# Attention: q and k of a steady turn are projected once, with even and odd columns crossed, and turned by adding halves of partitions

## The reference, cut to what matters

```
def rot(t):
    t = t.reshape(*t.shape[:-1], half, 2)
    t0, t1 = (t[..., 0], t[..., 1])
    r0 = t0 * cos - t1 * sin
    r1 = t1 * cos + t0 * sin
    return jnp.stack([r0, r1], axis=-1).reshape(*t0.shape[:-1], head_dim)
...
qkv = x @ qkv_w + qkv_b
...
q, k = _rope(q, k, S, D)
attn = jnp.einsum('bhqd,bhkd->bhqk', q, k) / math.sqrt(D)
attn = jax.nn.softmax(attn, axis=-1)
out = jnp.einsum('bhqk,bhkd->bhqd', attn, v)
return out @ out_w + out_b
```

## Time and profile before

| what | value |
|---|---|
| median of 3 runs | 1851.65 us |
| the profiled execution, first to last instruction (span) | 1847.4 us |
| so around the span | 4.25 us |
| TensorE's busy share of the span | 94% |
| VectorE, ScalarE, GpSimd | 78%, 76%, 77% |
| steady turns of the attention with a projection | 58 |

### The profile page before, as it was taken

How to read it: one execution, slowest core, us unless ns; L and a number is a source line. 1 busy time by engine, 2 the same in 40 slices (tenths; PEclk the granted TensorE clock), 3 DMA queues, 4 the chain that set the end, 5 groups by cost and what they waited for, 6 DMA issues and landing times. The chain is left out here.

```text
span 1847.4 us, 53971 instructions
## 1 busy us (share of the span) xinstructions
PE 1740.1 (94%) x22856; PEld 1101.7 (60%) x22856; DVE 1444.6 (78%) x2658; ACT 1407.5 (76%) x1737; POOL 1430.4 (77%) x851
## 2 busy tenths in 40 slices
PE   5999999999999999999999999986899999978997
PEld 2466666666666666666666666675556666653454
DVE  5888888888888888888888887535988888845785
ACT  2688888888888888888888888943998888853463
POOL 6699999999999999999999999974765566624122
PEclk9899999999999999999999999998999999989998
DMA  5101010111101010101010010050111111110000
GB/s 142 25 20 31 19 31 23 27 26 28 26 24 30 21 31 19 31 23 28 23 31 23 24 26 4 2 165 18 41 40 36 37 37 37 34 26 1 1 0 24
DMA packets 71080, 56.89 MB, mean 31 GB/s; under 512 B 29196, under 2 KB 64184, under 8 KB 70840
## 3 DMA queue, kind: packets, MB, share of 16 engines
q1 hardware_dynamic: 70840, 53.44, 11.5%
HBM read 14.54 MB, written 1.05 MB: 8 GB/s over the span
## 5 line engine op out<-in xcount | busy, mean ns | idle before, releaser
L278 POOL TENSOR_TENSOR ah_probs_lo<-ah_probs,ah_probs_hi 128x1024 f16<-128x1024 f32 x512 | 1072.8, 2132 | 78.8 <-ACT ah_probs L487 78.7
L542 DVE TENSOR_REDUCE ah_part_max<-ah_p_m 128x1 f32<-128x512 f32 x1024 | 669.2, 685 | 120.9 <-PE ah_p_m L342 111.1
L484 ACT ACTIVATE ah_probs_hi<-ah_p_s 128x1024 f16<-128x1024 f32 x512 | 531.2, 1038 | 190.0 <-PE ah_p_s L358 178.8
L487 ACT ACTIVATE ah_probs<-ah_p_s 128x1024 f32<-128x1024 f32 x512 | 532.4, 1040 | 0.0
L372 PE MATMUL ah_p_o<-ah_v_hi,ah_probs_hi 128*128 128x65 f16 x4096 | 470.5, 195 | 5.7 <-POOL ah_probs_lo L278 5.1
L374 PE MATMUL ah_p_o<-ah_v_lo,ah_probs_hi 128*128 128x64 f16 x4096 | 470.5, 193 | 0.0
L376 PE MATMUL ah_p_o<-ah_v_hi,ah_probs_lo 128*128 128x65 f16 x4096 | 470.3, 194 | 0.0
L372 PEld LDWEIGHTS ah_p_o<-ah_v_hi,ah_probs_hi 128*128 128x128 f16 x4096 | 383.0, 98 | 84.3 <-DVE a_attn L565 12.3
L374 PEld LDWEIGHTS ah_p_o<-ah_v_lo,ah_probs_hi 128*128 128x128 f16 x4096 | 378.4, 98 | 91.3
L342 PE MATMUL ah_p_m<-ah_k_hi_lo,ah_q_hi_twice 128*128 128x512 f16 x1024 | 393.9, 385 | 6.6 <-DMA ah_max_q_lo<-ah_lo 3.1
L357 PE MATMUL ah_p_s<-ah_q_hi_twice,ah_k_hi_lo 128*128 128x512 f16 x1024 | 388.6, 379 | 0.8 <-ACT ah_probs L487 0.4
(11 more groups left out here) (316 smaller groups left out, 3090.0 us busy)
## 6 DMA issues: line engine op xcount, KB each, us to landing
ba_v_skew<-ba_v_own SPq DMA_DIRECT2D x64, 129.0 KB, 2.3
ah_q_hi_twice<-ah_hi SPq DMA_DIRECT2D x128, 64.0 KB, 2.0
ah_k_hi_lo<-ah_hi SPq DMA_DIRECT2D x64, 64.0 KB, 1.9
ah_one_k_hi<-ah_hi SPq DMA_DIRECT2D x64, 64.0 KB, 2.0
ah_k_hi_lo<-ah_lo SPq DMA_DIRECT2D x64, 64.0 KB, 2.0
ah_max_q_lo<-ah_lo SPq DMA_DIRECT2D x64, 64.0 KB, 2.0
ah_w_head<-in_w_heads SPq DMA_DIRECT2D x16, 160.0 KB, 2.4
bw_rot<-in_rot SPq DMA_DIRECT2D x4, 512.0 KB, 10.3
```

The source lines that it names most:

```text
L278: pool.tensor_tensor(pl[:, p % RW, :, :], pb[:, p % RP, :, :], ph[:, p % RW, :, :], ALU.subtract).then_inc(lo_pool, 1)
L484: act.activation(ph[:, p % RW, :, :], p_s[:, p % 2, :, :], ACT.Exp, scale=HD ** -0.5)
L487: act.activation(pb[:, p % RP, :, :], p_s[:, p % 2, :, :], ACT.Exp, scale=HD ** -0.5).then_inc(exp_done, 1)
L542: dve.tensor_reduce(part[:, t, 2 * half + b:2 * half + b + 1], p_m[:, b, :], AX, ALU.max).then_inc(maxed, 1)
```

## The change

In the steady turns the 128 columns of a projection are crossed: 32 partitions each of q's even columns, k's odd columns, q's odd columns, k's even columns. Then what a partition needs from its partner stands 64 partitions away, in the same bank. One projection serves both products: step 0 projects (`W_CROSSED`) and multiplies by the sine into `rot`, step 1 multiplies by the cosine in place, step 2 adds `rot`'s upper half to `p_a`'s lower half (`cross_first`), and step 3 subtracts `rot`'s lower half from `p_a`'s upper half (`cross_second`). Rounding moves to steps 4 and 5, the row of maxima to step 6, the projection of v to step 7. Since q and k now lie in quarters, twelve DMAs of 32 partitions take the place of six of 64. The weights of a head have 7 x 64 columns for the first two heads, which also serve the early projections, and 3 x 64 after that; they had 5 x 64.

```
-W_COLS = 5 * HD
+QUAD = HD // 2
+W_COLS, W_LATER = 7 * HD, 3 * HD
...
+QE, KO, QO, KE = (slice(i * QUAD, (i + 1) * QUAD) for i in range(4))
...
+                    if g >= LEAD_G:
+                        sp.dma_start(ka[0:QUAD, to, cs], hi[KE, g % 2, :]).then_inc(spread[g % 2], 16)
+                        sp.dma_start(ka[QUAD:HD, to, cs], hi[KO, g % 2, :]).then_inc(spread[g % 2], 16)
...
                     if j == 0 and g <= LAST_G:
                         pe.wait_ge(vl_done, g)
-                        project(turned_bank(g), g, W_TURNED, turned_ready)
-                    if j == 1 and g <= LAST_G:
-                        pe.wait_ge(rot_done, g + 1)
-                        project(proj_bank(g), g, W_QK, proj_ready)
-                    if j == 5 and e + 1 < TURNS:
+                        project(proj_bank(g), g, W_CROSSED, proj_ready)
+                    if j == 6 and e + 1 < TURNS:
...
-                    if j == 6 and g <= LAST_G:
+                    if j == 7 and g <= LAST_G:
                         pe.wait_ge(mrow_ready, e + 2)
                         project_v(g)
...
+                def cross_sin(g):
...
+                    dve.scalar_tensor_tensor(rot[:, :], p_a[:, :], bqk[:, 2, h:h + 1], sin[:, chunk(g % QC)], ALU.add,
+                                             ALU.mult).then_inc(rot_done, 1)
...
+                def cross_cos(g):
+                    h = g // QC
+                    dve.wait_ge(rot_done, g + 1)
+                    dve.scalar_tensor_tensor(p_a[:, :], p_a[:, :], bqk[:, 2, h:h + 1], cos[:, chunk(g % QC)], ALU.add,
+                                             ALU.mult).then_inc(cos_done, 1)
+
+                def cross_first(g):
+                    dve.wait_ge(cos_done, g + 1)
+                    dve.tensor_tensor(p_a[0:HD, :], p_a[0:HD, :], rot[HD:P, :], ALU.add).then_inc(first_half, 1)
+
+                def cross_second(g):
+                    dve.wait_ge(cos_done, g + 1)
+                    dve.tensor_tensor(p_a[HD:P, :], p_a[HD:P, :], rot[0:HD, :], ALU.subtract).then_inc(r_done, 1)
...
                     if g <= LAST_G:
-                        if j == 0:
-                            rotate_sin(g)
                         if j == 1:
-                            rotate_cos(g)
-                        if j == 2:
-                            rotate_sum(g)
+                            cross_cos(g)
+                        if j == 3:
+                            cross_second(g)
                         if j == 4:
+                            high(g)
+                        if j == 5:
                             low(g)
...
-                        if j == 3:
-                            high(g)
+                        if j == 0:
+                            cross_sin(g)
+                        if j == 2:
+                            cross_first(g)
...
-                    if j == 5 and e + 1 < TURNS:
+                    if j == 6 and e + 1 < TURNS:
                         max_rows(e + 1)
```

More of the change, by code:

```diff
@@ L113 @@
 LEAD_M = 12
-W_COLS = 5 * HD
-W_TURNED, W_QK, W_V = slice(2 * HD, 4 * HD), slice(0, 2 * HD), slice(4 * HD, 5 * HD)
+QUAD = HD // 2
+W_COLS, W_LATER = 7 * HD, 3 * HD
+W_CROSSED, W_V, W_QK, W_TURNED = (slice(0, 2 * HD), slice(2 * HD, 3 * HD), slice(3 * HD, 5 * HD),
+                                  slice(5 * HD, 7 * HD))
+QE, KO, QO, KE = (slice(i * QUAD, (i + 1) * QUAD) for i in range(4))
 EXP_SHIFT = 12 * float(np.log(2.0)) * HD ** 0.5
@@ L147, in mha_heads @@
         wl = sc.sb("w_lo", [P, 2, W_COLS], F16)
-        bqk = sc.sb("bias_qk", [P, 2, HEADS])
+        bqk = sc.sb("bias_qk", [P, 3, HEADS])
         qa = sc.sb("q_hi_twice", [P, SETS, S], F16)
@@ L184, in mha_heads, with spread_after, w_cols @@
         spread = [sc.sem(f"spread{b}") for b in range(2)]
-        SPREAD = 6 * 16
+        SPREAD, SPREAD_CROSSED = 6 * 16, 12 * 16
         LAST_G = TURNS - 1
+        def spread_after(turns):
+            early = min(turns, LEAD_G // 2)
+            return SPREAD * early + SPREAD_CROSSED * (turns - early)
+        def w_cols(h):
+            return slice(0, W_COLS if h < 2 else W_LATER)
         def turned_bank(g):
@@ L222, in _ @@
                         sp.wait_ge(w_split, h + 1)
-                        sp.dma_start(w32[:, :], a["w_heads"][h + 1]).then_inc(w_in, 16)
+                        sp.dma_start(w32[:, w_cols(h + 1)], a["w_heads"][h + 1, :, w_cols(h + 1)]).then_inc(w_in, 16)
                     sp.wait_ge(hi_done, g + 1)
+                    if g >= LEAD_G:
+                        sp.dma_start(ka[0:QUAD, to, cs], hi[KE, g % 2, :]).then_inc(spread[g % 2], 16)
+                        sp.dma_start(ka[QUAD:HD, to, cs], hi[KO, g % 2, :]).then_inc(spread[g % 2], 16)
+                        sp.dma_start(kb[HD:HD + QUAD, to, cs], hi[KE, g % 2, :]).then_inc(spread[g % 2], 16)
+                        sp.dma_start(kb[HD + QUAD:P, to, cs], hi[KO, g % 2, :]).then_inc(spread[g % 2], 16)
+                        for half in range(2):
+                            at = half * HD
+                            sp.dma_start(qa[at:at + QUAD, to, cs], hi[QE, g % 2, :]).then_inc(spread[g % 2], 16)
+                            sp.dma_start(qa[at + QUAD:at + HD, to, cs], hi[QO, g % 2, :]).then_inc(spread[g % 2], 16)
+                        sp.wait_ge(lo_done, g + 1)
+                        sp.dma_start(ka[HD:HD + QUAD, to, cs], lo[KE, g % 2, :]).then_inc(spread[g % 2], 16)
+                        sp.dma_start(ka[HD + QUAD:P, to, cs], lo[KO, g % 2, :]).then_inc(spread[g % 2], 16)
+                        sp.dma_start(qb[HD:HD + QUAD, to, cs], lo[QE, g % 2, :]).then_inc(spread[g % 2], 16)
+                        sp.dma_start(qb[HD + QUAD:P, to, cs], lo[QO, g % 2, :]).then_inc(spread[g % 2], 16)
+                        continue
                     sp.dma_start(ka[0:HD, to, cs], hi[HD:P, g % 2, :]).then_inc(spread[g % 2], 16)
@@ L238, in split_weights @@
                         pool.wait_ge(v_ready, QC * (h - 1))
-                    pool.tensor_copy(wh[:, h % 2, :], w32[:, :]).then_inc(w_hi_done, 1)
+                    cols = w_cols(h)
+                    pool.tensor_copy(wh[:, h % 2, cols], w32[:, cols]).then_inc(w_hi_done, 1)
                     pool.wait_ge(w_hi_done, h + 1)
-                    pool.tensor_tensor(wl[:, h % 2, :], w32[:, :], wh[:, h % 2, :], ALU.subtract).then_inc(w_split, 1)
+                    pool.tensor_tensor(wl[:, h % 2, cols], w32[:, cols], wh[:, h % 2, cols],
+                                       ALU.subtract).then_inc(w_split, 1)
                 split_weights(0)
@@ L506, in rotate_cos @@
                                              ALU.mult).then_inc(cos_done, 1)
+                def cross_sin(g):
+                    h = g // QC
+                    dve.wait_ge(proj_ready, g + 1)
+                    dve.wait_ge(r_done, g)
+                    if g > LEAD_G:
+                        dve.wait_ge(first_half, g - LEAD_G)
+                    dve.scalar_tensor_tensor(rot[:, :], p_a[:, :], bqk[:, 2, h:h + 1], sin[:, chunk(g % QC)], ALU.add,
+                                             ALU.mult).then_inc(rot_done, 1)
+                def cross_cos(g):
+                    h = g // QC
+                    dve.wait_ge(rot_done, g + 1)
[7 more added lines that the diff above has]
+                    dve.tensor_tensor(p_a[HD:P, :], p_a[HD:P, :], rot[0:HD, :], ALU.subtract).then_inc(r_done, 1)
                 def rotate_sum(g):
@@ L514, in high @@
                     dve.wait_ge(r_done, g + 1)
-                    dve.wait_ge(spread[g % 2], SPREAD * (g // 2))
+                    dve.wait_ge(first_half, g - LEAD_G + 1)
+                    dve.wait_ge(spread[g % 2], spread_after(g // 2))
                     dve.tensor_copy(hi[:, g % 2, :], proj_bank(g)).then_inc(hi_done, 1)
@@ L2296, in _layouts @@
     turned = np.roll(order, HD // 2)
-    a["w_heads"] = c(np.concatenate([w[:, 0][..., order], w[:, 1][..., order], w[:, 0][..., turned],
-                                     w[:, 1][..., turned], w[:, 2]], -1).transpose(1, 0, 2))
+    even, odd = order[:HD // 2], order[HD // 2:]
+    crossed = lambda q, k: np.concatenate([q[..., even], k[..., odd], q[..., odd], k[..., even]], -1)
+    a["w_heads"] = c(np.concatenate([crossed(w[:, 0], w[:, 1]), w[:, 2], w[:, 0][..., order], w[:, 1][..., order],
+                                     w[:, 0][..., turned], w[:, 1][..., turned]], -1).transpose(1, 0, 2))
     b = i["L0_attn_qkv_b"].reshape(3, HEADS, HD)
-    a["b_qk"] = c(np.stack([np.concatenate([b[0][:, o], b[1][:, o]], -1).T for o in (order, turned)], 1))
+    a["b_qk"] = c(np.stack([*(np.concatenate([b[0][:, o], b[1][:, o]], -1).T for o in (order, turned)),
+                          crossed(b[0], b[1]).T], 1))
     a["b_v"] = c(b[2].reshape(HEADS * HD // P, P).T)
```

12 lines of the change are left out of this document (6 added, 6 removed).

## The result

The kernel after takes 1834.09 us (median of 4 runs, 1832.1 to 1835.21) against 1851.27 us before (4 runs, 1843.76 to 1852.67): a ratio of 0.9917, 95% interval 0.9900 to 0.9934. The profiled span fell by 15.6 us, from 1847.4 to 1831.8.

A forecast was written before the change was run, and what follows sets the result against it. TensorE was taken to bound the steady turns at 18.20 us; 17.44 without waits plus 0.32 of new waiting gives 17.76, saving 25.5 us over 58 turns less 0.5 at the start: 1827 us, range 1805 to 1836.

The forecast's parts named there:

- four moves: VectorE's cosine product, both halves and the reduction behind the second change start partition; held, they make TensorE wait 0.32 us a turn.
- Removed from TensorE: Three projection matmuls, 0.64 us a turn, and a 0.12 us wait go, leaving 17.44 us a turn without a new wait.
- the old wait: In step 3 before the change, TensorE waits 0.12 us for VectorE's reduction; claimed to go.
- Hidden work: SyncE's twelve DMA issues, 7.2 us a turn, and operations moved one step back were claimed to stay covered by other work.
- two passes: Slower rival: additions crossing halves take 1.20 us each instead of 0.60, giving a turn of 18.96 and 1896 us; chance 0.06.
- The rival in which the moves overlap: VectorE's operations that change partitions overlap their neighbours after all: turn 17.44 us, time 1808 us; chance 0.33.
- the eaten gain: Rival: a partition change costs 0.20 us, TensorE waits 0.76, the turn is 18.20 again and the time 1852 us; chance 0.06.
- The price of a move: Delay of a VectorE operation that changes start partition: taken as 0.09 us, waiting only for its predecessor to end; four make 0.36.
- 0.04 us to spare: First maxima of step 1 to second of step 4: VectorE's train 6.56 us against TensorE's 6.60, before partition changes are charged.
- upper bound of 0.14: Most that one VectorE partition change was taken to cost, from a sum waiting for its product: 0.80 us in place of 0.66.
- its own sign of being wrong: Forecast wrong if halves exceeded 0.8 us, TensorE stood elsewhere than step 4's second maxima, or the turn got to 17.4.
- The sum: Turn 17.44 + 0.32 = 17.76 us, 0.44 less; times 58, 25.5 us, less 0.5 at the start, 25.0; time 1827 us.

The follow-up runs named there:

- the run of halves that move nowhere: Against the kernel after, both halves work on partitions 0 to 63 of `p_a` and `rot`, so the result is no longer the rotation; 1811.98 us.
- the three and two of the experiments: Against the kernel after: second half first, in step 2, first half in step 3, 1827.17 us; or second half on partitions 0 to 63 of `p_a`, 1821.42 us.

## Why the prediction was right, and where a term was off

The mechanism forecast is there: less work for TensorE, and a train of VectorE that four moves make late, ahead of the second maxima of step 4. One term of it was too small, and a second wait was missed.

**Removed from TensorE**: three matmuls a turn and the old wait. Without a move the turn is 17.44 us, as summed (the run of halves that move nowhere). **Hidden work**: the halves are 0.69 and 0.71 us long on 64 partitions, as the sum was on 128 (0.69), so nothing goes in two passes; the twelve DMAs cost nothing against six. The rival in which the moves overlap falls by the rows, and the eaten gain by the size of the wait.

**The moves** are exactly the four named, and the three and two of the experiments. The rule of the Trainium skill, VectorE: DVE Perf Modes, section Two Vector instructions with no wait between them, names the same ones in each kernel. The traces agree: 0.70 to 0.74 us behind the operation in front for those, 0.59 to 0.61 for the reductions and halves that it lets start at once. **The price of a move is the term that was mis-sized**: 0.09 us was taken, as if the operation started at the end of the one in front; it starts 0.03 later. Four cost 0.47 instead of 0.36, and the wait in step 4 is 0.43 instead of 0.32. The 0.04 us to spare was a little small as well: three moves of 0.37 in all made a wait of 0.30, two of 0.23 one of 0.15. The mean, 0.12, lies midway to the upper bound of 0.14.

**A second wait was not forecast.** The train was summed up to the second maxima of step 4 and no further, and of the operations moved one step back the forecast checked the projection of v and the row of maxima, not the rounding. By its own sign of being wrong, TensorE standing at another place, it missed this one. Behind the first wait VectorE needs 605.29 - 603.16 = 2.13 us from the second reduction of step 3 to that of step 4, where TensorE, from the second maxima of step 4 to where that of step 5 would follow, takes 605.94 - 603.91 = 2.03. In that train the reduction at 604.09 starts 0.21 behind the negated maxima, since it waits for them (`m_done` in `reduce_max`).

A train longer than TensorE's side is no wait by itself. In the kernel before, these rows have the same stretch, behind the reductions that start at 610.39 in the earlier trace rows:

```profile
612.31 0.17 DVE L549 TENSOR_REDUCE ah_neg_max<-ah_part_max 128x4 f16<-128x16 f32 x1
612.39 0.69 DVE L516 CAST ah_hi<-ah_p_a 128x512 f16<-128x512 f32 x1
613.07 0.69 DVE L542 TENSOR_REDUCE ah_part_max<-ah_p_m 128x1 f32<-128x512 f32 x1
...
614.28 2.04 DVE L542 TENSOR_REDUCE ah_part_max<-ah_p_m 128x1 f32<-128x512 f32 x3
```

The last of those three starts at 611.58 and the second reduction of step 4 at 614.28, 2.70 us later, and TensorE doesn't wait, because the reduction at 611.58 lets it go on 0.74 later, at 612.32, and the maxima that need it come at 613.16. In the kernel after the first wait has used up all that was to spare, and the 0.10 by which the train is too long shows in full. Without a move, in the same order, it doesn't; with the rounding out of the train it doesn't either.

Whether the rounding's old place would have been enough is open, and no run tried it alone. There it follows the negated maxima in 0.08 us and fills part of the 0.21, but the reduction behind it came 0.68 later, not 0.60. By these rows the old order would save 0.04 to 0.13 us of the train, and 0.10 are needed.

**The sum.** 17.76 forecast, 0.11 for the moves and 0.09 for the second wait make 17.96. That both waits together, 0.52 us, equal the forecast's upper bound for the moves alone is luck. The turns give 0.245 x 58 = 14.2 us, in place of 25.5. The span shrank by 15.6: 0.9 up to the first steady projection (57.98 to 57.09 us), 14.6 from there to the last one, and the rest behind it. The medians differ by 17.2. Outside the steady turns single executions scatter by some us: the first steady projection stands anywhere from 57.1 to 58.7 us in the traces here, and from the attention's last weighing matmul to the end they take 629.7 to 634.6. The 0.5 us put down for the start can't be told from that. The time is 7 us above the forecast, and within its range by 2 us.

## What to carry to other kernels

When an in-order engine has little slack, sum its train not to the first consumer that gets late but to where it catches up, since behind a wait nothing is left to spare, and look for what an operation covered at its old place before moving it. An operation that changes the half of the partitions is cheap in itself, 0.10 to 0.14 us here, and costs that on the path only as far as it makes late what another engine waits for: with the second half, the rounding and the low part behind the reductions of their steps the four moves cost the turn nothing, and the same change gave 2.3% instead of 0.8%.

## What was not expected of the hardware

One changed start was enough, of each of three kinds: the cosine product begins late for its PSUM output alone (0.72 us behind its reduction, 0.61 where the operation ahead had written at 0), the halves of the run with two moves for their SBUF input alone (0.72 and 0.71), and the reduction behind the second half for its PSUM input alone (0.74; 0.60 or 0.61 where that had not moved). An output that moves in SBUF alone was not tried.
